# A graph network's second layer: two of eight attention heads' values weighed by ScalarE, six by VectorE

## The reference

```python
def _L1_gnn_ref(h, row, col, Wq, bq, Wk, bk, Wv, bv, Wo, bo):
    q = (h @ Wq.T + bq).reshape(N, HEAD_DIM, HEADS) * scaling
    k = (h @ Wk.T + bk).reshape(N, HEAD_DIM, HEADS)
    v = (h @ Wv.T + bv).reshape(N, HEAD_DIM, HEADS)
    s = jnp.einsum('edh,edh->eh', q[row], k[col])
    m = jax.ops.segment_max(s, row, num_segments=N)
    e = jnp.exp(s - m[row])
    z = jax.ops.segment_sum(e, row, num_segments=N)
    attn = e / z[row]
    out = jax.ops.segment_sum(attn[:, None, :] * v[col], row, num_segments=N)
    return out.reshape(N, -1) @ Wo.T + bo
```

## Time and profile before

| | |
|---|---|
| median of 3 runs | 8171.8 us (8169.69 to 8186.81) |
| span of the profiled execution, first to last instruction | 8112.0 us |
| second layer's edge pass, first to last exponential L1622 | 2853.8 to 3636.1 us |
| busy in the span: PE, DVE, ACT, POOL | 69%, 50%, 35%, 39% |

### The profile page before, as it was taken

How to read it: one execution, slowest core, us unless ns; L and a number is a source line. 1 busy time by engine, 2 the same in 40 slices (tenths; PEclk the granted TensorE clock), 3 DMA queues, 4 the chain that set the end, 5 groups by cost and what they waited for, 6 DMA issues and landing times. The chain is left out here.

```text
span 8112.0 us, 86982 instructions
## 1 busy us (share of the span) xinstructions
PE 5601.5 (69%) x21290; PEld 3555.5 (44%) x21290; DVE 4057.9 (50%) x9795; ACT 2838.0 (35%) x7825; POOL 3138.4 (39%) x3209
## 2 busy tenths in 40 slices
PE   2222547677699778887785568698857866888576
PEld 1111325445355356653343345354545543555343
DVE  5325836665311389994434333423456675555501
ACT  4223627664122144430102333122246633555110
POOL 3663035553466166640005662100056634555011
PEclk9999965557799878778997778799956666787588
DMA  2221521111010255540002221100033423333122
GB/s 84 69 65 42 173 66 43 40 39 16 26 32 20 74 157 159 160 129 14 8 27 87 84 85 39 38 33 30 14 103 106 110 66 92 89 91 90 54 109 69
DMA packets 272398, 573.85 MB, mean 71 GB/s; under 512 B 87398, under 2 KB 138138, under 8 KB 265242
## 3 DMA queue, kind: packets, MB, share of 16 engines
q0 software_dynamic: 134496, 314.63, 15.5%
q1 hardware_dynamic: 137530, 254.96, 9.6%
HBM read 520.14 MB, written 49.19 MB: 70 GB/s over the span
## 5 line engine op out<-in xcount | busy, mean ns | idle before, releaser
L1288 POOL DMA_INDIRECT L_edges_rows<-scratch_L_kv,L_edges_index x416 | 491.1, 1180 | 392.5 <-PE L_edges_ps_sum L1533 221.5
L1288 POOL DMA_INDIRECT L3a_edges_rows<-scratch_L3a,L3a_edges_index x416 | 442.6, 1064 | 472.7 <-DMA L3a_edges_last<-order_dst_last 256.7
L1288 POOL DMA_INDIRECT L3b_edges_rows<-scratch_L3b,L3b_edges_index x416 | 396.8, 954 | 460.1 <-PE L3b_edges_ps_sum L1533 296.7
L1288 POOL DMA_INDIRECT L_edges_rows<-scratch_L,L_edges_index x416 | 416.4, 1001 | 372.2 <-DVE L_edges_msg L1335 199.2
L1730 POOL TENSOR_TENSOR L_norm_fold<-L_norm_square 128x400 f32<-128x400 f32 x64 | 66.5, 1040 | 1262.2 <-ACT L_norm_square L1739 1262.2
L676 POOL DMA_INDIRECT L_edges_rows<-scratch_L,L_edges_index x416 | 396.8, 954 | 394.2 <-SPq L660 145.6
L499 POOL DMA_INDIRECT scratch_by_dst<-dst_record,dst_dest x400 | 406.2, 1016 | 315.0 <-DVE dst_dest L338 195.6
L518 POOL DMA_INDIRECT scratch_by_src<-src_record,src_dest x400 | 387.7, 969 | 266.9 <-issue 110.1
L688 PE MATMUL L_edges_ps_sum<-L_edges_rows,L_edges_hot 128*128 128x256 f32 x832 | 271.1, 466 | 222.7 <-issue 122.8
L400 PE MATMUL rank_ps_count<-rank_parts,rank_ident_b 128*128 128x225 bf16 x200 | 53.6, 370 | 534.6 <-DVE rank_parts L312 423.9
L2376 DVE TENSOR_TENSOR L_experts_gated_h<-L_experts_hidden,L_experts_share_rows 128x800 f32<-128x800 f32 x112 | 111.0, 992 | 609.5 <-ACT L_experts_hidden L2366 535.0
(11 more groups left out here) (761 smaller groups left out, 13494.6 us busy)
## 6 DMA issues: line engine op xcount, KB each, us to landing
x<-scratch_dst_key_rows SPq DMA_DIRECT2D x50, 512.0 KB
x<-scratch_src_key_rows SPq DMA_DIRECT2D x50, 512.0 KB
L_experts_w<-in_L_w SPq DMA_DIRECT2D x16, 1024.0 KB
L_edges_rows<-scratch_L,L_edges_index POOLq DMA_INDIRECT x832
L_edges_lo_rows<-order_src_lo_rows SPq DMA_DIRECT2D x52, 256.0 KB
L3a_edges_lo_rows<-order_dst_lo_rows SPq DMA_DIRECT2D x52, 256.0 KB
L3b_edges_lo_rows<-order_dst_lo_rows SPq DMA_DIRECT2D x52, 256.0 KB
x<-scratch_dst_lo_rows SPq DMA_DIRECT2D x50, 256.0 KB
```

Of the source, the lines that this page charges most:

```text
L1288: pool.indirect_dma_start(rows[:, n % RING, k, 0:RW], None, row_table, bass.IndirectOffsetOnAxis(index[:, t:t + 1].bitcast(U32), 0)).then_ ...
```

## The change

One number differs: in the "dot" form `act_heads` is 2 where it was 0. ScalarE's `weigh` then issues 16 activations of 128x32 per batch (eight tiles, two heads), each a copy scaled by the head's weight. VectorE's L1391 covers heads 2 to 7. TensorE's `sums` waits, for the first tile of a batch, on both engines' semaphores (L1528 to L1531) instead of VectorE's alone.

```diff
     PARTS = 3 * H
     HALF = RW // 2
-    act_heads = {"dual": 3, "dot": 0, "add": 2 if H > 1 else 1}[kind]
+    act_heads = {"dual": 3, "dot": 2, "add": 2 if H > 1 else 1}[kind]
     buckets = order["buckets"]
```

## The result

The changed kernel takes 8267.65 us (median of 4 runs, 8262.53 to 8288.0), the kernel before 8178.18 us beside it (8169.69 to 8186.81): ratio 1.0104, 95% interval 1.0082 to 1.0125, slower by 67 to 102 us. The prediction was 8241 with 8205 to 8290. On another chip, where the kernel before takes 7295.94, the ratio was 1.0112 (1.0095 to 1.0129).

The account below looks back on a forecast made before the run. Bound taken: a loop through VectorE, ScalarE's copy, TensorE's pairs and the scan, 15.34 us a batch. Terms: 61.0 for 50 batches, 0.5 for the end, 7.3 for TensorE's clock, 68.8 in all; 8241 us, range 8205 to 8290.

Parts of the forecast that it names:

- The loop: Second layer's edge pass: exponentials to first copy 7.40, to scan 3.03, to next exponentials 6.04; 16.47 us a batch.
- The first leg: From the exponentials to ScalarE's first query copy: 7.40 us where it was 5.99, after 2.14 of slack is used up.
- Sixteen activations in 3.4 us: ScalarE's weighing, ahead of the one-hot matrix: 128x32 activations 0.212 us apart, 3.4 in all, bounds 3.0 and 3.83.
- the estimate in the prediction: Rival on ScalarE's activations not overlapping: 16 x 0.327 = 5.2 us by the skill's budget, time 8332; chance 0.02.
- VectorE's gain hidden: VectorE's weighing gets 0.54 us shorter, but this turns into idle time before the scan, about 2 us a batch.
- "None of the pairs" at the lower clock: TensorE's pairs 2 and 3, behind the first copies, keep full clock in every batch and take 1.99 us.
- the earliest start of the sums: TensorE reaches the sums 3.64 us after the exponentials at the earliest; waiting for ScalarE's weighing loses at most 0.4, hidden.
- The rival: TensorE's pairs 2 and 3 fall to the lower clock, 1.63 us more each batch; 8341 if all, 8287 if half; chance 0.09.
- More third legs at the lower clock: Scan to next exponentials: a third more of the batches take 6.48 us, +7.3 us; ends nothing and 26.
- The end: Last two batches: the one without copies gains 0.54 us, the last loses some 1.0 waiting for ScalarE; +0.5 together.
- upper end: Forecast's own upper end: 1.65 us a batch from a later copy, plus 26 for clock, 8281; widened to 8290.

Follow-up runs that it names:

- ScalarE's part alone: Against the changed kernel: VectorE weighs all eight heads again, ScalarE's sixteen activations write key numbers nobody reads; 7370.57 us, ratio 1.0106 to the kernel before.
- the changed kernel's second profile: The changed kernel run once more, unaltered, as yardstick on the chip where the kernel before takes 7295.94; 7370.42 us, ratio 1.0112.

## Why the prediction was right, and where it was not

- *The loop* (three legs through VectorE, ScalarE's copy, TensorE's pairs, the scan) was right. The first leg was predicted at 7.40 and is 7.28; the copy starts 0.09 before L1600's end, not 0.03 after it. That is -6 us.
- *Sixteen activations in 3.4 us*: 3.41 (3498.42 to 3501.83), 0.213 apart. The line through 64 and 128 columns held at 32. The budget of the Trainium skill ("ScalarE: Activation LUTs", Rules for kernel authors: 0.3 us and 0.83 ns for each element) would have made it 5.2, by the estimate in the prediction. One activation does take 0.307 by itself here, but in a run of them the next starts before that.
- *VectorE's gain hidden*: right. The instruction was predicted at 1744 ns and takes 1748, the idle time ahead of the scan at 1.5 to 2 us and is 1.74; ScalarE's part alone gave the whole loss.
- *"None of the pairs" at the lower clock*: this step failed. 13 batches of 50 had them, 1.89 us each, +24.6 us. The ground given, that TensorE works nearly without a pause up to the sums, held for the three batches shown. It does not hold in a batch that begins at full clock: pairs 0 and 1 end 2.16 us after the exponentials there, the sums' new wait ends at 4.2, and the clock falls under the sums, before the copy's wait. I had put the earliest start of the sums at 3.64 by one row and the loss at 0.4; before the change the earliest of the 50 was 2.94, in the 3 batches that began at full clock, so the trace of before had it and three batches in a row did not show it. The rival had the kind of event, but blamed the gap right ahead of the pairs, had too small a chance, and was priced for half of the batches or all.
- *More third legs at the lower clock*, +7.3: wrong in sign, 6.16 went to 6.11. Against the 6.28 of the sum that is -8.4 us.
- *The end*: the batch without copies was predicted at -0.54 and gave -1.10 (-0.50 in the changed kernel's second profile: it differs from run to run). The last sums start 4.21 instead of 2.91 after the exponentials, +1.3 where 1.0 was predicted; that lies behind the pass.

Of the 68.8 predicted, 67.8 lie in the pass. With -6 for the first leg, +24 for the second, -8.4 for the third and -0.6 for the end this makes 76.8, against 77.1 measured. The further 12 us between pass and medians (89.5) lie within the interval and outside the changed code; they were not followed, and on the other chip the medians differ by 74.5 only. The range held, and partly by luck: its upper end was made of a later copy and of slower third legs, and the room was used by the slow pairs, for which the sum had nothing. Errors of the other sign cancelled 15 of their 24 us.

## What to carry to other kernels

Before work is moved to an engine that looks idle, find the next thing on that engine that others wait for, and read its slack in front of it: here 2.1 us per batch. The slack shrinks by what the relieved engine gains, 0.27 us for each head (L1391 takes 2.01 us with seven heads, 2.28 with eight). So there was room for one head (1.7 us, 21 us faster) and not for two (3.4 us, 75 to 90 slower); ScalarE's share of 42% told neither. Where the work must go there, pull the hand-over ahead of what nobody waits for yet: that alone turned the two-head kernel from 75 us slower to 16 faster. Putting the work behind the hand-over was not run, nor one head together with the early copies. The shortest pass found is the one with a single head on ScalarE (759.2, against 767.4 with two heads and early copies); the intervals of these two kernels' times overlap.

## What the runs showed of the hardware that was not expected

- Idle time of TensorE was paid twice: the wait for the copy, 1.3 us in the mean, in every batch, and 1.89 us more in the 13 where the clock had fallen before the pairs. Giving TensorE 1.30 us of needless work per batch (at full clock), ahead of the wait of the sums, took the slow pairs from 13 to none.
- The same program takes about 8180 us on some chips and 7295 on others. Part of it is the ranking stage at the start, whose last L464 ends at 1001 us in the profile of before and at 601 in that of the changed kernel's second run; the waits of the former have rows that end "remote", up to 38 us long, and the latter none among its longest:

```profile
DVE x L318 <- remote: 349.0, 22, 37.7
ACT rank_apart L464 <- remote: 239.1, 22, 27.8
```

What is behind them was not looked into.
